# An attention block on one core: TensorE's order in each step of two slots goes from scores, large products, value products to scores, value products, large products

## What is computed

```
h = group_norm(xf, norm_scale, norm_bias)        # statistics over all 1024 tokens of the image
qkv = h @ qkv_w + qkv_b                          # [16, 1024, 1536]
q, k, v = split(qkv, 3, axis=-1)
q = (q * scale).reshape(bs * 8, 1024, 64)        # a plain reshape of (1024, 512)
weight = softmax(einsum('btc,bsc->bts', q, k))
a = einsum('bts,bsc->btc', weight, v)
h = a.reshape(bs, 1024, 512) @ proj_w + proj_b
return xf + h
```

## Time and profile before

| | |
|---|---|
| time, median of 3 runs (lowest, highest) | 3559.65 us (3553.75, 3564.28) |
| the profiled execution's own time | 3560.03 us |
| its span, first to last instruction | 3558.1 us |
| mean granted TensorE clock | 0.995 |
| busy: TensorE, its weight loads, DVE, ACT, POOL | 98%, 71%, 78%, 58%, 46% |
| share of the span that TensorE holds in the chain that ended last | 91% |
| DMA engines: queue that carries the moves | 75.5% of 16 engines' span |

### The profile page before, as it was taken

One profiled execution on the slowest core, in us unless ns is written; L12 is line 12 of the kernel. 1 busy time (PEld: TensorE's weight loads), 2 busy tenths in 40 slices (PEclk: granted clock), 3 DMA queues, 4 the chain that ended last, 5 costly groups with the idle time before them and its releaser, 6 DMA issues.

```text
span 3558.1 us, 77277 instructions
## 1 busy us (share of the span) xinstructions
PE 3471.5 (98%) x24640; PEld 2523.3 (71%) x24640; DVE 2792.0 (78%) x3473; ACT 2062.7 (58%) x3985; POOL 1627.2 (46%) x2762
## 2 busy tenths in 40 slices
PE   6999999999999999999999999999999999999998
PEld 5777777677677776777777777777777777777775
DVE  5878878788787787878878787787877878788776
ACT  5556556565565665655555656555556556565563
POOL 4355444444454454444535445444444444454452
PEclk9999999999999999999999999999999999999999
DMA  4778778777787877777777777777877778787776
GB/s 127 190 182 190 184 181 192 178 189 182 182 190 176 189 184 186 184 178 192 178 188 184 182 189 182 183 182 184 191 175 183 186 179 191 175 189 186 178 179 169
DMA packets 255884, 648.50 MB, mean 182 GB/s; under 512 B 73872, under 2 KB 73872, under 8 KB 255376
## 3 DMA queue, kind: packets, MB, share of 16 engines
q1 hardware_dynamic: 254224, 638.35, 75.5%
q10 hardware_dynamic: 1152, 4.19, 0.3%
HBM read 71.84 MB, written 33.55 MB: 30 GB/s over the span
## 4 chain that ended last, share of the span: by engine, by line
PE 91%; issue 3%; POOL 2%; ACT 2%; DVE 1%; SPq 1%; DMA 0%; POOLq 0%; ACTq 0%
PE pv_ps L411 26%; PE s_ps L381 21%; PE c_ps L451 7%; PE c_ps L452 6%; PE c_ps L453 6%; PE c_ps L434 4%; PE c_ps L462 4%; PE c_ps L463 3%; PE c_ps L464 3%; PE c_ps L436 3%; PE c_ps L435 3%; PE pv_ps L392 2%; PE s_ps L484 2%; ACT staged L531 1%; SPq L344 1%
## 5 line engine op out<-in xcount | busy, mean ns | idle before, releaser
L644 DVE TENSOR_REDUCE neg_max<-s_ps 128x1 f32<-128x1024 f32 x1024 | 1205.1, 1218 | 674.6 <-PE s_ps L381 674.3
L513 ACT ACTIVATE probs<-s_ps,neg_max 128x1024 f32<-128x1024 f32 x1024 | 1143.5, 1117 | 978.6 <-DVE neg_max L644 974.9
L627 DVE STREAM_TRANSPOSE turned<-probs 128x1024 f32<-128x1024 f32 x1024 | 1231.9, 1227 | 47.2 <-ACT probs L513 7.0
L411 PE MATMUL pv_ps<-probs_t,v 128*64 128x256 f32 x8192 | 1000.6, 386 | 9.8 <-DMA probs_t<-turned 9.8
L411 PEld LDWEIGHTS pv_ps<-probs_t,v 128*64 128x64 f32 x8192 | 545.8, 137 | 347.1 <-issue 117.2
L451 PE MATMUL c_ps<-h_hi,w_hi 128*128 128x256 f32 x2048 | 606.7, 296 | 10.2 <-POOL h_lo L754 6.4
L452 PE MATMUL c_ps<-h_lo,w_hi 128*128 128x256 f32 x2048 | 579.4, 283 | 0.0
L453 PE MATMUL c_ps<-h_hi,w_lo 128*128 128x256 f32 x2048 | 579.1, 283 | 0.0
L531 ACT ACTIVATE staged<-c_ps,qk_bias 64x256 f32<-64x256 f32 x1024 | 479.9, 469 | 18.6 <-PE c_ps L453 5.3
L451 PEld LDWEIGHTS c_ps<-h_hi,w_hi 128*128 128x128 f32 x2048 | 391.1, 191 | 102.7 <-issue 96.4
L767 POOL CAST qh_e<-staged 128x256 fp32r<-128x256 f32 x256 | 102.4, 400 | 643.8 <-ACT staged L531 643.8
(11 more groups left out here) (71 smaller groups left out, 5187.4 us busy)
## 6 DMA issues: line engine op xcount, KB each, us to landing
probs_t<-turned SPq DMA_DIRECT2D x4096, 128.0 KB, 2.3
x_res<-in_x SPq DMA_DIRECT2D x128, 256.0 KB, 2.7
result<-x_res SPq DMA_DIRECT2D x128, 256.0 KB, 2.0
x_next<-in_x SPq DMA_DIRECT2D x120, 256.0 KB, 2.7
probs_t<-in_L_conv_qkv_w ACTq DMA_DIRECT2D x4, 768.0 KB, 8.9
turned<-in_x SPq DMA_DIRECT2D x4, 512.0 KB, 12.9
probs_t<-in_L_conv_proj_w ACTq DMA_DIRECT2D x4, 256.0 KB, 13.8
v_bias<-in_L_conv_qkv_b SPq DMA_DIRECT2D x1, 256.0 KB, 16.9
```

The source lines that it names most:

```text
L411: last = nc.tensor.matmul(pv_ps[side][CH * par:CH * (par + 1), 0, :], v_sb[:, ring_of(i, parity), CH * chunk:CH * (chunk + 1)], p_t[:, par ...
L513: nc.scalar.activation(probs[k % 2][:, :], s_ps[k % 2][:, :], ACT.Exp, bias=neg_max[:, k % 4:k % 4 + 1], accum_out=row_sum[:, (k // HALF) ...
L627: nc.vector.transpose(dst, probs[k % 2][:, :].rearrange("p (k b j) -> p k b j", k=CHUNKS, b=QUADS)).then_inc(probs_turned, 1)
L644: nc.vector.tensor_reduce(neg_max[:, k % 4:k % 4 + 1], s_ps[k % 2][:, :], AX.X, ALU.max, negate=True).then_inc(max_ready, 1)
```

## The change

The lag at which the value products of a half run goes from 9 slots to 8, and the calls in `slot` change places. The first part of a half (with the spread) moves from slot 4n+9 to slot 4n+8, the second from 4n+11 to 4n+10. Each stays in the same step of two slots, but now stands right behind the scores of that step and ahead of the large and small products of both its slots. No instruction is added or removed, and no other engine's program changes.

```diff
-ATTEND_LAG = 9
+ATTEND_LAG = 8
...
                 if k % 2 == 0 and within(s, N_SLOTS):
                     scores(b, k)
                     scores(b, k + 1)
-                large(b, k)
-                small(b, k)
                 if k % HALF == ATTEND_LAG % HALF and within(s - ATTEND_LAG, N_SLOTS):
                     spread_inverse(b, k)
                     attend(b, k, 0)
                 if k % HALF == (ATTEND_LAG + 2) % HALF and within(s - ATTEND_LAG - 2, N_SLOTS):
                     attend(b, k - 2, 1)
+                large(b, k)
+                small(b, k)
```

## The result

| | before | changed |
|---|---|---|
| time, median (lowest, highest) | 3559.65 us (3553.75, 3564.28) | 4090.13 us (4087.54, 4091.23) |
| span of the profiled execution | 3558.1 us | 4085.6 us |
| mean granted TensorE clock | 0.995 | 0.953 |

The change makes the kernel slower by 15%: ratio 1.1496, 95% interval 1.1467 to 1.1525. The forecast was 4030 in 3930 to 4120.

What follows compares the result with a forecast made beforehand. TensorE, busy 98% of the span, bounds the kernel, so each new wait adds its full length. Terms 229+111+11+18+25+71 = 465 on 3559.65 gave 4025, said as 4030; range 3930 to 4120.

Steps and rivals of the forecast that it cites:

- steps (1) to (4): Delay chain from step 4 through DVE, ACT and POOL to step 8's spread: widening 0.83 later, TensorE stands 4.10.
- Steps (1) and (2): Step 4: DVE's maxima start at T+2.1, not T+1.01; exponentials move by 1.1, ACT free for staging at T+5.6.
- The moves: DMA moves of turned halves: zero cost, 0.4 to spare; as rival, landing 1 us late per pair, 4090, chance 0.07.
- The spread, 229 and 11: Step 8 waits for POOL's widening: 3.64 x 63 = 229; ACT's copy in slot 37 adds 0.76 x 15 = 11.
- The clock, 71: Half clock behind step 8's new pauses: 1.4 us in four of five of 63 pairs, 71 us; bounds 0 and 170.
- the worst case of 2.7: Costliest half-clock stretch behind an image-end pause, at 2667.61: 2.7 us in its step; upper bound 63 x 2.7 = 170.
- near 0.97: Sign that the prediction is right: mean granted TensorE clock near 0.97 in the changed kernel.
- The rival in which the clock falls in every pair: Each step 8 wait costs 1.4 to 2.7, 126 us in place of 71: 4080 to 4125; chance 0.15.
- Copies of x, 111: Scores wait for ACT's copy of transposed x, small products being last in the step: 0.93 x 119 = 111 us.
- Group averages, 18: TensorE waits for DVE's group averages, small products being last in the step: 0.6 x 30 = 18; bounds 0 and 28.
- Large products later: ACT, DVE and POOL get large products' units 2 us later; outside steps 4 to 8 nobody waits: zero.
- Order switches, 25: Spread behind scores instead of large products: 0.13 more per spread, x 193 = 25 us; bounds 0 and 50.

Runs made afterwards that it cites:

- experiment 1: Changed kernel, but POOL widens the reciprocals ahead of the query split in the same slot: 3862.15 us, ratio 1.0862.
- experiment 2: Changed kernel, but POOL widens one slot earlier (slot 6, not 7) and ahead of that slot's split: 3693.56 us, ratio 1.0387.
- experiment 10: Changed kernel, but DVE takes values of slots 0 and 1 and each projection behind both transposes of its step: 4041.99 us, ratio 1.1362.
- experiment 6: Kernel before, TensorE order unchanged, with only POOL's widening moved to slot 6 ahead of that slot's split: 3553.63 us, ratio 0.9996.
- experiment 4: Changed kernel with 32 extra matmuls on TensorE ahead of the wait for the widening in step 8: 3959.66 us, ratio 1.1135.
- experiment 9: Changed kernel with widening in slot 6 before the split, small products before large, DVE's value and projection takes behind both transposes: 3570.17 us, ratio 1.0038.
- experiment 7: Kernel before, with the new order only in the last step of each image (slots 62 and 63): 3526.7 us, ratio 0.9919.

## Why the prediction was right, and which terms were off

**Right in mechanism and order.** The largest term was the spread that waits for POOL's widening in step 8, 63 times: shown by experiments 1 and 2, which changed nothing but POOL's order. The chain of steps (1) to (4) held: 2.1, 5.6, 12.07 and 18.6 behind step 4's start were named, 1.93, 5.65, 12.09 and 18.61 measured. That the binding link is query tile 2's own product and not the exponentials was shown by experiment 10. Steps (1) and (2), DVE's lateness of 1.1 and what follows from it, happened but cost nothing here: the staging of step 4 starts at 5.65 with them and without them. The pause, named 4.10, was 4.00; in the pair with a copy of x in step 4 it was 4.71, so 0.71 for the 0.76 named. The moves never came next (experiment 2), and nobody on TensorE waited for staged units elsewhere.

**Sizes that were off**, by the terms of the sum:

- *The spread, 229 and 11.* The pauses grew by 263.1 less 4.5, or 259 us. "Less the wait of about 0.46 that it has there today ... x 63" failed: only one step in four had that wait in full (experiment 6). The 240 was 19 too small.
- *The clock, 71.* "1.4 in four of five pairs" was mis-sized: half clock followed in all 63 pairs, and cost 1.9 in each, 121 (experiment 4, by steps), between the 1.4 and the worst case of 2.7. The granted clock was 0.953, not "near 0.97". The pause of 4.47 from which I took 1.4 was followed by one group of value products; here large products follow, and in the stretches shown above some of them are slow too. The rival in which the clock falls in every pair, 126 for this term, was the case that came.
- *Copies of x, 111.* 120 waits came, and the price was 0.8, not 0.93: about 95. The 0.93 took nothing off for what the steps pay anyway: steps 0, 12, 16, 28 and 36 grew by 0.97, 1.00, 0.88, 0.91 and 0.99 in the median, and 0.16 of that is the spread's dearer place.
- *Group averages, 18.* They cost 57, of which 33 are the 30 waits themselves (27.6 and 5.2). "0.6 x 30" was read off a place where DVE had nothing else to do. In an image DVE takes the first average behind both transposes, and is late by the take that waits and by the statistics (experiments 9 and 10); 1.88 per image, and then 2.04 in step 46, of which some 1.6 is half clock. So the zero of "Large products later" failed here: the late take of the projection reaches TensorE through the average, for 1.1 of the 1.88 (experiment 9).
- *Order switches, 25.* 0.13 foreseen, 0.16 measured, 31 for 193 spreads.
- *The image's end.* Named nowhere; 34 us the other way. The pause is 26 us shorter over the images (experiment 7 shows it alone), and in 5 of 13 images of the kernel before it was followed by half clock, which made step 0 8.5 to 9.7 us long and not 7.1, together 8.5; none is left. I had read that pause only as a sample of the clock.

259 + 121 + 95 + 57 + 31 - 34 = 529 against 531 by steps. What the forecast left out or sized too small (+50, +39, +19, +6) is partly cancelled by what it sized too large or did not see (-16, -34); the total came as near as it did (4030 for 4090) with some luck, and is no proof of each part.

## What to carry to other kernels

When one engine's work is moved ahead inside a step, look at each semaphore it waits on and ask what stands ahead of the releasing instruction in that engine's queue; here a 0.4 us copy behind two unrelated splits cost 397 us, and moving that copy cost nothing. What had stood ahead of the moved work was covering somebody's latency: list what followed it (here two hand-backs of a PSUM bank). And price a pause of TensorE in a dense kernel with the slow stretch behind it, by the work that follows there.

## What the runs showed that I had not expected

- Useless matmuls in a pause that can't be avoided made the kernel 130 us faster (4090.13 to 3959.66), at a granted clock of 0.995 instead of 0.953.
- The pause at a loop's end on TensorE depends on what stands last in the body. With 12 large matmuls of 512 columns last (0.23 us from start to start) it is 0.2 to 0.8 us in the changed kernel and 0 to 1.1 in the other versions that end so, with 16 value matmuls last (0.12 each) 2.1 to 3.0. The reading that the slower matmuls cover a fixed time at the loop's end fits, but was only argued; no run here varied the last instructions further.
- Longer pauses were followed by half clock more often: those of 1.6 to 1.75 us in 5 of 47 cases, those of 2.44 in 13 of 14 (both experiment 1), those of 3.8 and more in 63 of 63 (changed kernel). But the length alone doesn't decide: the same pause of 1.85 ahead of step 46 was followed by it in 14 of 15 images of the changed kernel (value products of 3.30 at 1243.23) and in 8 of 15 in experiment 2, and pauses of 2.1 to 3.0 in the kernel before in 5 of 13.
